# FFN products with plain fp32 operands in place of two fp32r parts, and later tiles' keys and values made at the head of the first tile

## What is computed

```python
x = x + xattn(layernorm(x), ctx)      # 8 heads of 32, causal mask, biases on q, k, v, out
x = x + ffn(layernorm(x))

def ffn(x):                           # weights w are ternary (-1, 0, 1), s is a scale per output
    h = silu(tlin(x, w1, s1)) * tlin(x, w2, s2)      # 256 -> 1024
    h = gelu(tlin(h, h1, h1s))                       # 1024 -> 1024
    h = gelu(tlin(h, h2, h2s))                       # 1024 -> 1024
    return tlin(h, w3, s3)                           # 1024 -> 256
```

## Time and profile before

| | us |
|---|---|
| median of 3 runs | 1544.83 |
| lowest, highest | 1544.02, 1545.79 |
| profiled execution | 1543.65 |
| its span | 1541.9 |
| PE busy | 1532.9 |
| DVE busy | 802.0 |
| ACT busy | 697.2 |
| POOL busy | 123.1 |

### The profile page before, as it was taken

One profiled execution on the slowest core, in us unless ns is written; L12 is line 12 of the kernel. 1 busy time (PEld: TensorE's weight loads), 2 busy tenths in 40 slices (PEclk: granted clock), 3 DMA queues, 4 the chain that ended last, 5 costly groups with the idle time before them and its releaser, 6 DMA issues.

```text
span 1541.9 us, 21318 instructions
## 1 busy us (share of the span) xinstructions
PE 1532.9 (99%) x8422; PEld 1249.0 (81%) x8422; DVE 802.0 (52%) x1276; ACT 697.2 (45%) x1013; POOL 123.1 (8%) x134
## 2 busy tenths in 40 slices
PE   9999999999999999999999999999999999999998
PEld 6787888888888887888888888887888888888887
DVE  6664735547354474644548354474644547354332
ACT  4653534436354453534536354353634536354342
POOL 1001011010100201001010100201001010100000
PEclk9999999999999999999999999999999999999999
DMA  9951020212202121020212202121030211202000
GB/s 377 347 189 50 32 84 27 75 48 65 57 14 77 53 67 49 31 85 27 75 41 64 65 14 75 55 67 49 24 92 27 75 41 64 64 16 68 14 1 15
DMA packets 50529, 106.32 MB, mean 69 GB/s; under 512 B 9026, under 2 KB 24394, under 8 KB 47690
## 3 DMA queue, kind: packets, MB, share of 16 engines
q1 hardware_dynamic: 50506, 106.00, 21.1%
HBM read 61.93 MB, written 32.52 MB: 61 GB/s over the span
## 4 chain that ended last, share of the span: by engine, by line
PE 96%; DMA 1%; SPq 1%; DVE 0%; ACT 0%; issue 0%; ACTq 0%
PE ffn_banks L479 84%; PE att_banks L660 4%; PE att_banks L602 3%; PE att_banks L619 2%; PE att_banks L650 2%; DMA h_bits<-in_h 1%; PE att_banks L670 1%; SPq L370 1%; PE ffn_banks L693 0%; ACT junk L725 0%; SPq L349 0%; PE ffn_banks L685 0%; DVE inexact L861 0%; PE att_banks L590 0%; DVE a_lo L887 0%
## 5 line engine op out<-in xcount | busy, mean ns | idle before, releaser
L479 PE MATMUL ffn_banks<-b_hi,h_sb 128*128 128x512 f32 x1024 | 404.4, 395 | 0.0
L479 PE MATMUL ffn_banks<-b_lo,h_sb 128*128 128x512 f32 x1024 | 399.0, 390 | 0.0
L479 PE MATMUL ffn_banks<-a_hi,h_sb 128*128 128x512 f32 x1024 | 398.3, 389 | 0.0
L479 PE MATMUL ffn_banks<-a_lo,h_sb 128*128 128x512 f32 x1024 | 398.3, 389 | 0.0
L759 ACT ACTIVATE a_f<-ffn_banks,vec 128x512 f32<-128x512 f32 x128 | 88.2, 689 | 367.1 <-PE ffn_banks L479 367.1
L887 DVE TENSOR_TENSOR a_lo<-a_f,a_hi 128x512 fp32r<-128x512 f32 x128 | 94.5, 739 | 298.0 <-ACT a_hi L760 297.9
L479 PEld LDWEIGHTS ffn_banks<-b_hi,h_sb 128*128 128x128 f32 x1024 | 192.3, 188 | 45.1 <-issue 6.2
L479 PEld LDWEIGHTS ffn_banks<-a_hi,h_sb 128*128 128x128 f32 x1024 | 192.2, 188 | 39.9
L479 PEld LDWEIGHTS ffn_banks<-a_lo,h_sb 128*128 128x128 f32 x1024 | 192.2, 188 | 39.9
L479 PEld LDWEIGHTS ffn_banks<-b_lo,h_sb 128*128 128x128 f32 x1024 | 192.3, 188 | 38.9
L479 PE MATMUL ffn_banks<-ln_hi,w_sb 128*128 128x512 f32 x512 | 203.6, 398 | 0.6 <-DVE v_later L915 0.6
(11 more groups left out here) (103 smaller groups left out, 1580.9 us busy)
## 6 DMA issues: line engine op xcount, KB each, us to landing
blocks_dram<-blocks SPq DMA_DIRECT2D x30, 512.0 KB, 3.0
attn_t<-blocks_dram SPq DMA_DIRECT2D x60, 256.0 KB
h_bits<-in_h SPq DMA_DIRECT2D x8, 1024.0 KB, 19.1
h_sb<-h_bits SPq DMA_DIRECT2D x8, 1024.0 KB, 8.5
out<-out_sb SPq DMA_DIRECT2D x32, 256.0 KB, 2.0
x_in<-in_x SPq DMA_DIRECT2D x15, 512.0 KB, 3.6
ln_t<-in_x_t SPq DMA_DIRECT2D x14, 512.0 KB, 4.4
ln_rows<-ln_rows_dram SPq DMA_DIRECT2D x14, 512.0 KB, 4.0
```

Source lines behind the costliest of these rows:

```text
L479: mm = nc.tensor.matmul(psum, left, right, start=(k == 0 and part == 0), stop=(k == rows - 1 and part == 1))
```

## The change

1. FFN operands and weights are plain fp32. `product` is gone; one matmul stands for each pair. The casts, the second gelu and all subtractions to lo go.
2. CHECK, COUNT, FLAG, READ, KEEP and the general program go: weight pieces are loaded once, and there is one program.
3. In the loop, T2 leaves PE. DVE transposes LN2's rows in 32x32 blocks behind LN2A, XW writes them to DRAM, XR reads them to `ln2_t` in four DMAs, which puts the tokens in another order inside the tile; the last gelu (L3) writes its rows back in the order of L4. T2 stays in the head.
4. In `ORDER` one L2 block moves behind PV, and the LN2 steps stand one L3 block earlier.
5. In the head, two KX and two VX steps stand before K of tile 0, and the other ones are spread anew; their loads come first; the keys' and values' weights are loaded apart.
6. Buffers: `blocks`, `tail_blocks`, `ln1_rows` and `row_blocks` lie over `k_later`, so DVE's first DT waits for the spilled keys, where ACT waited before; `attn_t` has its own place, so that MV waits for the stores of the tile before only.

```diff
 ORDER = [
...
+    ("L1", 4), ("L1", 5), ("L1", 6), ("L1", 7), ("EXP", 0), ("MASK", 1), ("MAX", 1), ("SUB", 1), ("EXP", 1),
+    ("SOFT", 0), ("DT", 0), ("L2", 0), ("SOFT", 1), ("DT", 1), ("L2", 1), ("MV", 0), ("L2", 2), ("MV", 1),
+    ("L2", 3), ("L2", 4), ("L2", 5), ("L2", 6), ("PV", 0), ("PV", 1), ("L2", 7),
+    ("L3", 0), ("O", 0), ("CTX", 0), ("LN2S", 0), ("L3", 1), ("LN1S", 0), ("LN2A", 0), ("XW", 0), ("ROWS", 0), ("XR", 0),
+    ("L3", 2), ("L3", 3), ("L3", 4), ("LN1A", 0), ("L3", 5), ("L3", 6), ("L3", 7), ("Q", 0), ("L4", 0), ("L4", 1),
 ]
...
 FIRST = [
+    ("KX", 0, 0), ("KX", 1, 0), ("KD", 0, 0), ("KD", 1, 0), ("VX", 0, 0), ("VD", 0, 0), ("VX", 1, 0), ("VD", 1, 0),
     ("K", 0, 0), ("T1", 0, 0), ("V", 0, 0), ("LN1S", 0, 1), ("Q", 0, 0), ("XLN", 0, 1),
+    ("KX", 2, 0), ("S", 0, 0), ("MASK", 0, 0), ("MAX", 0, 0), ("KD", 2, 0), ("KX", 3, 0), ("S", 1, 0),
+    ("SUB", 0, 0), ("MASK", 1, 0), ("MAX", 1, 0), ("EXP", 0, 0), ("KD", 3, 0), ("KX", 4, 0), ("KX", 5, 0), ("KD", 4, 0), ("KD", 5, 0),
+    ("SUB", 1, 0), ("T1", 0, 1), ("KX", 6, 0), ("EXP", 1, 0), ("KD", 6, 0), ("VX", 2, 0), ("BIAS", 0, 0),
+    ("SOFT", 0, 0), ("VD", 2, 0), ("VX", 3, 0), ("SOFT", 1, 0), ("VD", 3, 0), ("PT", 0, 0), ("PT", 1, 0), ("KX", 7, 0), ("KX", 8, 0),
+    ("KD", 7, 0), ("KD", 8, 0), ("PT", 2, 0), ("PT", 3, 0), ("VX", 4, 0), ("PV", 0, 0), ("PV", 1, 0), ("CTX", 0, 1), ("VD", 4, 0),
+    ("VX", 5, 0), ("VD", 5, 0), ("O", 0, 0),
+    ("Q", 0, 1), ("ADD", 0, 0), ("LN2S", 0, 0), ("VX", 6, 0), ("VD", 6, 0), ("K", 0, 1), ("V", 0, 1),
+    ("LN2A", 0, 0), ("BIAS", 0, 1), ("VADD", 0, 1), ("T2", 0, 0),
+    ("VX", 7, 0), ("VD", 7, 0), ("VX", 8, 0), ("VD", 8, 0),
+    ("SPILL", 0, 0), ("SPILL", 1, 0),
 ]
...
@@ SP
+                    if step == "XW":
+                        sp.wait_ge(rows_blocked, t)
+                        sp.dma_start(row_blocks_dram.rearrange("k p b i -> p k (b i)"), row_blocks[:].rearrange("p k b i -> p k (b i)"))\
+                            .then_inc(row_blocks_out, 16)
+                    if step == "XR":
+                        sp.wait_ge(row_blocks_out, 16 * t)
+                        sp.wait_ge(up_ready, KH * f + KH)
+                        for b_ in range(4):
+                            src = row_blocks_dram[:, :, b_, :].rearrange("k (r f) i -> f (k r) i", r=4)
+                            dst = ln2_t[32 * b_:32 * b_ + 32].rearrange("f k (r i) -> f (k r) i", r=4)
+                            sp.dma_start(dst, src).then_inc(ln2_there, 16)
...
@@ SP, loads at the start
+            sp.dma_start(w_att_sb[:, 1], w_att[:, 1]).then_inc(k_w_loaded, 16)
+            load_later_ctx(0)
             sp.dma_start(x_in[:], x_tiles[0]).then_inc(x_loaded, 16)
+            sp.dma_start(vec[:, 0:n_small], vectors[:, 0:n_small]).then_inc(vec_loaded, 16)
+            sp.dma_start(w_att_sb[:, 2], w_att[:, 2]).then_inc(v_w_loaded, 16)
+            sp.dma_start(vec[:, n_small:n_small + D], vectors[:, n_small:n_small + D]).then_inc(bv_loaded, 16)
             load_ctx(0)
-            sp.dma_start(w_att_sb[:, 1:3], w_att[:, 1:3]).then_inc(kv_w_loaded, 16)
...
@@ PE
                         if n == 0:
-                            pe.wait_ge(ln2t_done, f + 1)
-                            pe.wait_ge(w_kept, 32)
+                            pe.wait_ge(ln2_there, 64 * f + 64)
+                            pe.wait_ge(piece_loaded[0], 16)
+                            pe.wait_ge(piece_loaded[1], 16)
                             pe.wait_ge(kx_done, 2 * NG - 1)
+                            pe.wait_ge(vx_done, (NCH + 1) // 2 - 1)
...
+                            for k in range(KD):
+                                mm = nc.tensor.matmul(fb[:, 2 * (n % 2) + i, :], w_sb[:, k, n * P:(n + 1) * P], ln2_t[:, k, :],
+                                                      start=(k == 0), stop=(k == KD - 1))
...
+                        for k in range(KH):
+                            if n == 0:
+                                pe.wait_ge(piece_loaded[first_piece + k // 2], 16)
+                            if n == 0 and (k == 0 or k >= at_once):
+                                pe.wait_ge(rows_done, KH * f + max(k + 1, at_once))
+                            mm = nc.tensor.matmul(fb[:, n % 4, :], w_sb[:, k, n * P:(n + 1) * P], rows[:, k, :],
+                                                  start=(k == 0), stop=(k == KH - 1))
...
+                            for k in range(KH):
+                                if j == 0 and (k == 0 or k == KH - 1):
+                                    pe.wait_ge(gelu3_done, KH * f + max(k + 1, KH - 1))
+                                mm = nc.tensor.matmul(fb[:, 2 + n, i * D:(i + 1) * D], a_sb[:, k, j * P:(j + 1) * P], w3_sb[:, k, :],
+                                                      start=(k == 0), stop=(k == KH - 1))
...
             pe.wait_ge(id_ready, 1)
-            spin(20)
-            pe.wait_ge(kv_w_loaded, 16)
+            spin(12)
+            pe.wait_ge(k_w_loaded, 16)
...
@@ DVE
                     if step == "DT":
                         dve.wait_ge(probs_ready, NB * t + n + 1)
+                        if n == 0:
+                            dve.wait_ge(k_spilled[0], 32)
+                            dve.wait_ge(k_spilled[1], 16 * (NG - 2))
...
                         ln_apply(x1, 1, t)
+                        if f is not None:
+                            dve.wait_ge(ln_ready[1], t + 1)
+                            for k in range(KD):
+                                op = nc.vector.transpose(row_blocks[:, k, :, :],
+                                                         xln[:, :, k * P:(k + 1) * P].rearrange("p j (b f) -> p b j f", b=4))
+                            op.then_inc(rows_blocked, 1)
```

More of the change, by code:

```diff
@@ L154, in build_kernel @@
[L154 to L162, removed]
@@ L167, in build_kernel @@
+        put("later_rest", [P, 512])
+        c_later, _ = put("c_later", [P, KD * LATER], at=later_at)
+        v_later, _ = put("v_later", [P, NCH, D], at=later_at + 4 * KD * LATER)
+        assert later_at + 4 * KD * LATER + 4 * NCH * D <= top[0]
+        k_later, k_later_at = put("k_later", [P, HG * LATER])
+        q_t, _ = put("q_t", [P, HG, TILE])
+        ln2_t, _ = put("ln2_t", [P, KD, TILE])
+        attn_t, _ = put("attn_t", [TK, H, TQ])
         w_att_sb, _ = put("w_att_sb", [P, 4, KD, D])
@@ L205, in build_kernel @@
         warm, _ = put("warm", [P, 1])
+        marks, _ = put("marks", [P, 3])
         eps, _ = put("eps", [P, NQ])
         minus_half, _ = put("minus_half", [P, NQ])
[L208 to L212, removed]
         rows_dram = nc.dram_tensor("ln1_rows_dram", (2, TILE), F32, kind="Internal").ap()
@@ L295, in later_keys @@
             return k_later[:, HG * GROUP * g:HG * (GROUP * g + group_width(g))].rearrange("p (m n) -> p m n", m=HG)
-        def general_chunks(step, n):
-            if step == "L1":
-                return [w[:, k, n * P:(n + 1) * P] for w in (w1, w2) for k in range(KD)]
-            if step in ("L2", "L3"):
-                w = h1 if step == "L2" else h2
-                return [w[:, k, n * P:(n + 1) * P] for k in range(KH)]
-            if step == "L4":
-                return [w3[:, k, c * P:(c + 1) * P] for _ in range(2) for c in range(KD) for k in range(KH)]
-            return []
-        CHUNKS = sum(len(general_chunks(s, n)) for s, n in ORDER if s in FFN)
-        chunk_base = {}
-        at = 0
-        for s, n in ORDER:
-            if s in FFN:
-                chunk_base[s, n] = at
-                at += len(general_chunks(s, n))
         block = es.enter_context(nc.Block())
@@ L529, in one_pass @@
+                            mm.then_inc(ready, 1)
                     if step in ("L2", "L3"):
-                        w_sb, src_hi, src_lo, h_done, ready, own = (
-                            (h1_sb, a_hi, a_lo, h1_done, l2_ready, gelu2_done) if step == "L2"
-                            else (h2_sb, b_hi, b_lo, h2_done, l3_ready, gelu3_done))
+                        w_sb, rows, rows_done, ready, own, first_piece, at_once = (
+                            (h1_sb, a_sb, up_used, l2_ready, gelu2_done, 2, 1) if step == "L2"
+                            else (h2_sb, b_sb, gelu2_done, l3_ready, gelu3_done, 6, KH - 3))
@@ L663, in one_pass @@
                         mm.then_inc(o_ready, 1)
-                    if step == "T2":
+                    if step == "T2" and f is None:
                         pe.wait_ge(ln_ready[1], t + 1)
-                        if f is None:
-                            pe.wait_ge(q_done, 2)
+                        pe.wait_ge(q_done, 2)
                         for k in range(KD):
@@ L697, in one_pass @@
                         spin(n)
-                    if step == "FLAG":
-                        pe.wait_ge(row_summed, 1)
-                        nc.tensor.matmul(fb[0:1, 3, 0:1], inexact_row[:], ones[:], start=True, stop=True).then_inc(flag_summed, 1)
-                    if step == "READ":
```

(24 more changed lines are left out.)

259 lines of the change are left out of this document (61 added, 198 removed), and 14 rows, old and new, of tables (FIRST, ORDER).

## The result

The changed kernel takes 2655.9 us (four runs, 2655.89 to 2656.14) against 1544.6 us: a ratio of 1.719, 95% interval 1.716 to 1.722. The forecast was 2654, range 2632 to 2684. The span of the profiled execution is 2654.1 us.

The account below looks back on a forecast made before the run. PE bounds the kernel throughout: 1541.9 us span, plus 1114 for the tiles (15 x 69.6 + 70.4), minus 3.6 in the head, gives 2652.3; with 1.75 around the span 2654 us, range 2632 to 2684.

Parts of the forecast that it names:

- The bound: Whole kernel: PE busy 1532.9 of 1541.9 us, so time follows PE's instructions, plus the head, plus any new wait.
- Two instructions a product, twice the columns each: FFN products: a plain fp32 product is two instructions, 0.429 us each for 512 columns, 0.2163 for 256; instruction count unchanged.
- The tile period: Each loop tile: FFN from 80.4 to 151.1 us, net +69.6 with T2 gone, period near 162.4 us.
- allowance of -0.3 for edges: Each tile, between unlike PE instructions: -0.3 us taken, between bounds of -0.8 and +0.3.
- The head: Before the first FFN product: three things move, net -3.6 us, bounds -6 and +5.
- The start: Head: PE's first real work moves from 8.32 to 5.7 us as fewer bytes load first, -2.6 us.
- The waits: Head: FLAG, READ, the last wait for DVE and part of the wait for the probabilities go, -1.5 us.
- The microsecond for late values' weights: Head: early VX needs weights queued behind 1.5 MB, up to a microsecond late, counted as +0.5 us.
- The way over DRAM: LN2's rows in the loop: a chain of about 15 us stays hidden under 51 us of cover.
- the rival: New wait in every tile, LN2's rows late over DRAM: 1 us a tile gives 2670, 5 us 2730; 7%.
- Half price: FFN: a plain 512-column product takes 0.429 us, under the pair's 0.455, giving 1446 us; 2%.
- Loads in the open: FFN: weight loads of 0.189 us for each of 384 instructions exposed, 73 us a tile, 3815 us; 1%.

## Why the prediction was right, step by step

- **The bound.** PE in each stage: right, no wait of PE in the loop. DVE and ACT came out at 20 and 17% busy, where I had put them near a quarter.
- **Two instructions a product, twice the columns each.** Right: 5120 instructions, 0.4301 and 0.2158 us against my 0.429 and 0.2163. Shown to be the cause by the run with the form alone.
- **The tile period.** 92.78 + 69.6 = 162.4 foreseen, 162.61 measured. T2 gave 0.88 instead of 0.79 us. My allowance of -0.3 for edges was a guess between bounds. It came out so: at 0.4301 and 0.2158 us the FFN takes 151.4 us, 71.0 more than before, less 0.88 for T2, and 69.8 was measured. The part behind the head, 1116.9, is 3 us above my 1114, and the 0.001 us by which I had the spacing too short is more than that.
- **The head.** The sum was near (-3.6 against -4.7), its terms were not. The start: I had the old one set by the landing of the weights, but the earlier trace rows have no wait at 8.32: the 40 spin instructions ended half a microsecond behind the load, and it took both, fewer spins and earlier loads, to get to 6.94. I put the first KX at 5.7 us, it was 6.94: the 24 spins ended at 6.5 us (1.63 + 4.85), and the load came 0.46 us behind them. I had priced the 24 at the mean of the 40, 0.167 us, but the first ones are slower: in the kernel before, too, only 24 have begun by 6.5 us, all at granted clock 1.00. The waits: I took 1.5 us of them away; all of them went, with the check's product and edges, 3.3 us. The microsecond for late values' weights didn't come. Two misses of 1.2 and 2.3 us partly cancelled, and the 1.1 us left over ran against the 3 us of the loop, so that my span of 2652.3 is only 1.8 us short. Both were luck.
- **The way over DRAM.** Right that it is hidden: 178.2 against a need at 225.77, 47 us to spare where I had 36. The price of the rival is now measured: 4.85 us of wait and 2.8 us of lower clock a tile once the cover is down to 7 us. I had priced the wait alone.
- **The rivals.** Half price: refuted by the count and by the spacing. With it falls the one-half factor of the Trainium skill's Perfetto Trace Analysis (Engine Utilization, footnote 1), read as the cost of a whole fp32 product, for which the rows show twice that. Four passes, as the Trainium skill's FP8 and Floating Point Precision (TensorE Precision Notes) has it, is what the rows give: 0.860 us for a product of 512 columns, where four times 512 columns at 2.4 GHz are 0.853. Loads in the open: refuted by the cut products.

## What to carry to other kernels

Before you exchange an operand's type, find a product of the new type and the same shape in the old trace, and read its price start to start, with the number of instructions that it becomes: one fp32 product of 512 columns is two instructions of 0.43 us, an fp32r pair two of 0.227. Here one engine was the bound throughout, and adding such rows up gave a change of 70% within 0.1%, with some luck in the small terms. With half the FFN work the same sum was 435 us short, since that engine waited, and hidden chains and the clock set the time. Work that leaves the bound engine (T2) is worth having in either form; price the cover of what replaces it before moving it later.

## What I had not expected of the hardware

- An fp32r instruction costs a fixed 13 ns above its columns at 2.4 GHz, in a pair (0.2267 for 512 columns, by the 127 steps from 85.03 to 113.82 us in the kernel before; 0.1198 for 256) and, within what that short stretch tells, alone (0.231); plain fp32 ones cost about 2 to 3 ns above twice their columns. Why is open.
- Weight loads shown as 0.19 us can stream at one per 0.112 us.
- Waits of 0.8 and 1.7 us close together, and one of 4.85 us alone, were each followed by instructions at the lower clock; waits of 1.21 and 0.69 us, 2.6 us apart in the same head as the first two, were not (clock 1.00 from 42 to 50 us). The changed kernel, with no wait in the loop, stayed at 1.00.
